# Keys, beta, gram products and block solve of the delta rule moved one period up, into a stream of their own

## The reference, cut to what matters

```python
xn = layernorm(x)
# layer 0: delta rule (4 heads, dk 128, dv 32) beside a two-layer network
q, k, v = xn @ Wq, xn @ Wk, xn @ Wv; beta = sigmoid(xn @ Wb); g = xn @ Wg
k = k * rsqrt(sum(k * k) + 1e-12)
#   S_t = S_{t-1} + k_t (beta_t (v_t - k_t^T S_{t-1}))^T ;  o_t = q_t^T S_t
o = norm(o) * silu(g)
x = x + o @ Wo + ffn(xn)       # ffn: 2 layers of window-64 attention (8 heads) and a GELU MLP
xn = layernorm(x)
# layer 1: latent attention, 16 heads of 8, causal, beside 6 experts (top 2) and a shared expert
x = x + latent_attention(xn) + moe(xn)
```

## Time and profile before

| | |
|---|---|
| median of 3 runs | 2267.91 us (2267.54 to 2269.87) |
| profiled execution | 2270.01 us, span 2268.0 us |
| PE, PEld busy | 1957.7, 1291.3 us |
| DVE, ACT, POOL busy | 1401.9, 947.8, 824.7 us |
| mean granted TensorE clock | 0.91 |
| HBM traffic | 32 GB/s over the span |

### The profile page before, as it was taken

The page is one execution under the profiler, slowest core; times in us unless marked ns, Lnnn a source line. Parts: engine busy times, 40 slices in busy tenths (PEclk is TensorE's granted clock), DMA queues, the critical chain, the costliest instruction groups (busy, mean ns, idle before and its releaser), DMA issues. The chain is left out here.

```text
span 2268.0 us, 40783 instructions
## 1 busy us (share of the span) xinstructions
PE 1957.7 (86%) x15104; PEld 1291.3 (57%) x15104; DVE 1401.9 (62%) x3394; ACT 947.8 (42%) x2465; POOL 824.7 (36%) x823
## 2 busy tenths in 40 slices
PE   3797779998899988998899988998799988998686
PEld 1594448564685557654585557654585556754332
DVE  3553465775758756775757756775767847674442
ACT  1413442365424652265424643265514653264023
POOL 4506550444406541443506542353505442160000
PEclk9788898999899998999899998999999998999557
DMA  4200012100311012200302012100212012100200
GB/s 167 50 20 15 17 35 62 53 14 15 77 36 41 18 40 61 53 14 15 78 24 54 18 38 64 53 14 11 71 31 57 14 31 74 47 16 1 75 1 6
DMA packets 124820, 89.71 MB, mean 40 GB/s; under 512 B 42168, under 2 KB 111928, under 8 KB 124344
## 3 DMA queue, kind: packets, MB, share of 16 engines
q1 hardware_dynamic: 124016, 85.39, 14.0%
q0 software_dynamic: 320, 1.05, 0.1%
q10 hardware_dynamic: 288, 0.67, 0.1%
HBM read 46.84 MB, written 25.17 MB: 32 GB/s over the span
## 5 line engine op out<-in xcount | busy, mean ns | idle before, releaser
L1636 POOL TENSOR_TENSOR soft<-soft,prec 128x512 f32<-128x512 f32 x128 | 135.7, 1066 | 541.6 <-DVE prec L1295 540.5
L1163 ACT ACTIVATE shared<-bank 128x512 f32<-128x512 f32 (+1 forms) x384 | 202.7, 528 | 254.3 <-PE bank L931 252.3
L1447 DVE TENSOR_REDUCE nmx<-bank 128x1 f32<-128x512 f32 (+3 forms) x352 | 224.6, 638 | 105.3 <-PE bank L909 104.4
L1083 ACT ACTIVATE soft<-bank,nmax 128x128 f32<-128x128 f32 x512 | 180.2, 384 | 169.4 <-DVE nmax L1287 168.7
L1597 POOL TENSOR_TENSOR qk_rs<-qk_rs,minus_half 128x16 f32<-128x16 f32 x64 | 187.8, 2935 | 5.3
L930 PE MATMUL bank<-b_sb 128*128 128x128 bf16 x512 | 118.0, 231 | 41.6 <-ACT shared L1163 39.7
L931 PE MATMUL bank<-shared 75*128 75x384 bf16 (+3 forms) x512 | 149.5, 318 | 0.0
L621 PE MATMUL bank<-w_sb,hT 128*128 128x512 f32 x256 | 136.7, 620 | 8.7 <-DVE hT L1237 5.7
L909 PE MATMUL bank<-shared 72*128 72x256 bf16 (+3 forms) x512 | 135.9, 317 | 0.0
L1595 POOL TENSOR_SCALAR rs_f<-mv_f 128x4 f32<-128x4 f32 x24 | 5.6, 234 | 344.2 <-DVE mv_f L1226 344.2
L593 PE MATMUL bank<-c_sb,soft 128*128 128x128 f32 x608 | 106.3, 308 | 27.5 <-POOL soft L1636 22.4
(11 more groups left out here) (236 smaller groups left out, 4809.1 us busy)
## 6 DMA issues: line engine op xcount, KB each, us to landing
shared<-parts_dram SPq DMA_DIRECT2D x64, 288.0 KB
vm<-v_f SPq DMA_DIRECT2D x112, 128.0 KB, 2.3
parts_dram<-parts SPq DMA_DIRECT2D x96, 128.0 KB, 2.5
L_dram<-shared SPq DMA_DIRECT2D x32, 256.0 KB, 2.5
shared<-X_dram SPq DMA_DIRECT2D x32, 256.0 KB, 3.0
shared<-L_dram SPq DMA_DIRECT2D x32, 256.0 KB, 3.8
w_sb<-weights SPq DMA_DIRECT2D x1, 4167.0 KB, 21.2
x_tm<-x SPq DMA_DIRECT2D x8, 256.0 KB, 3.1
```

The lines of the kernel that those rows point to most:

```text
L1083: a = af(v4(p_sb, 2, 4)[:, j, g], place("fS", j)[:, g * P:(g + 1) * P], ACT.Exp, bias=nmax[:, at:at + 1], accum_out=psums[:, at:at + 1])
L1163: af(v4(PTm, 2, GROUP)[:, u % 2, i, 0:n], place("mST")[:, 0:n], ACT.Exp).then_inc(mexp_done, 1)
L1447: reduce(v3(nmx[:], HM)[:, h:h + len(heads), c], v3(place("mS")[:, 0:len(heads) * (c + 1) * P], len(heads)), AX, ALU.max, negate=True).the ...
L1636: tt(p, p, spread(prec[:, at:at + NPAIR], P), ALU.mult).then_inc(fnorm_done, 1)
```

## The change

A new stream e ("early") holds, for item p+1 in period p: the head (x load, layernorm, transpose), `k`, `krs`, `beta`, `kT`, `gram`, `solve` and `keep`. The delta stream of item p now begins with `qT` and `bg` and goes on with the inversion. Item 0's early steps stand alone before period 0, and period 7 has none. To live beside the latent attention, kT, kn and the blocks of the solve get tiles of their own outside `shared`, L is written into `the` (the experts' tile), and `k`, `beta`, `kT` and `gram` all use PSUM bank 3, each waiting for the readers of the one before. Beta is computed by four products of 4 columns with one tanh; the gate `bg` by four products into one bank with one tanh and one multiply. `xnT` of the next item is written in the middle of the period, and the shifted copy `hT` later, from `xnT` (`hcopy`). `qT`'s four copies come first on ACT. The zeroing of `X_dram` moves from POOL's queue to SP's, behind the weight loads. All five order strings are new. In the PE order the e steps stand so: `hT` between `seq_u(p,1)` and `seq_o(p,1)`; `k` to `gram` spread over the last 77 of 307 steps, with three `mST`, one `mPV`, `matg`, `aT` and `final` behind the last gram. `inv_v(p,0,0)` stands 14th instead of 53rd. On DVE, `solve` stands behind the last `matg` and ahead of `final` and of the next period's first `fS`; on SP, `solve` and `keep` stand ahead of `final`.

```diff
-STREAMS = "fbdacm"
+STREAMS = "fbdacme"
 def steps_front(b):
-    return s + (steps_head(b + 1) + steps_chunks(b + 1, 0, 0, AHEAD) if b + 1 < BATCH else [])
+    return s + ([("hcopy", b + 1)] + steps_chunks(b + 1, 0, 0, AHEAD) if b + 1 < BATCH else [])
+def steps_early(b):
+    s = (steps_head(b) if b else []) + [("k", b, c) for c in range(NT)] + [("krs", b), ("beta", b)] + [("kT", b, c) for c in range(NT)]
+    return s + [("gram", b, c) for c in range(NT)] + [("solve", b), ("keep", b)]
 def steps_delta(b):
-    s = [("k", b, c) for c in range(NT)] + [("krs", b)] + [("bg", b, c) for c in range(NT)]
-    s += [("kT", b, c) for c in range(NT)] + [("gram", b, c) for c in range(NT)]
-    s += [("qT", b, h) for h in range(H0)] + [("solve", b)]
+    s = [("qT", b, h) for h in range(H0)] + [("bg", b)]
...
-            "k": lambda c: c % 2, "bg": lambda c: c % 2, "kT": lambda c: c % 2, "G": lambda c: c % 2,
+            "k": lambda c: 3, "beta": lambda: 3, "kT": lambda c: 3, "G": lambda c: 3, "bg": lambda: 0,
...
+        kT, kn, blk = sb("kT", NT * T), sb("kn", NT * T), sb("blk", 3 * BLK * BLK)
+        Lx = the
...
                 def gram(b, c):
                     kc = v4(kT, NT, H0)[:, c]
-                    pe.wait_ge(kT_copied, NT * b + min(c + 3, NT))
-                    if c >= 2:
-                        pe.wait_ge(L_done, NT * b + c - 1)
+                    if c:
+                        pe.wait_ge(L_done, NT * b + c)
+                    else:
+                        pe.wait_ge(kT_copied, NT * (b + 1))
...
+                def hcopy(b):
+                    dve.wait_ge(head_copied, b + 1)
+                    if b:
                         dve.wait_ge(fv_psum, ch(b, 0, 0))
-                    nc.vector.tensor_copy(xnT[:], place("hT")[:])
-                    nc.vector.tensor_copy(hT[0:64, :], place("hT")[0:64, :])
-                    nc.vector.tensor_copy(hT[64:P, 1:T], place("hT")[64:P, 0:T - 1]).then_inc(head_copied, 1)
+                    shifted(hT, xnT).then_inc(hT_copied, 1)
...
                 def inv_load(b, c):
                     if c == 0:
-                        keep(b)
-                    sp.wait_ge(Xb_kept, 16 * (b + 1))
+                        sp.wait_ge(Xb_kept, 16 * (b + 1))
+                        if b:
+                            sp.wait_ge(oT0_copied, b)
+                        if b > 1:
+                            sp.wait_ge(mPV_psum, GROUPS * 3 * (b - 1))
```

More of the change, by code:

```diff
@@ L204, in period @@
     if p < 0:
-        return {s: steps_head(0) + steps_chunks(0, 0, 0, AHEAD) if s == "f" else [] for s in STREAMS}
+        first = {"f": steps_head(0) + [("hcopy", 0)] + steps_chunks(0, 0, 0, AHEAD), "e": steps_early(0)}
+        return {s: first.get(s, []) for s in STREAMS}
     early, late = p < BATCH, p > 0
@@ L215, in walk @@
         left = {s: collections.deque(x for x in steps if x[0] in parts) for s, steps in period(p).items()}
-        for s in ORDER[engine]:
+        for s in ORDER[engine] if p >= 0 else [s for s in STREAMS for _ in left[s]]:
             if left[s]:
@@ L294, in build @@
         warm, minus_half = sb("warm", 2), sb("minus_half", 16)
-        kss, krs, beta = sb("kss", NT * H0), sb("krs", NT * H0), sb("beta", NT * H0)
+        kss, krs, beta, bt = (sb(n, NT * H0) for n in ("kss", "krs", "beta", "bt"))
         oss, ors = sb("oss", NT * H0), sb("ors", NT * H0)
@@ L517, in _ @@
                 sp.dma_start(c_sb[:, early_c:], consts[:, early_c:]).then_inc(late_loads, 16)
+                sp.wait_ge(zeroed, 2)
+                for c in range(NT):
+                    sp.dma_start(in_dram(X_dram, c), v3(zeros, H0)).then_inc(X_zeroed, 16)
+                sp.wait_ge(X_zeroed, 16 * NT)
                 sp.wait_ge(setup_loads, 16 * 3)
@@ L1150, in delta_back @@
                     af(o_all, place("o")[:], ACT.Copy).then_inc(o_back, 1)
-                    af(kn[:, 0:T], place("o")[:], ACT.Square).then_inc(osq_done, 1)
+                    af(Vm[:, 0:T], place("o")[:], ACT.Square).then_inc(osq_done, 1)
                 def oT0_(b):
@@ L1375, in gram @@
                     for h in range(H0):
-                        m = stt(v4(L, 2, H0)[:, c % 2, h], v3(place("G", c)[:], H0)[:, h], beta[:, c * H0 + h:c * H0 + h + 1],
+                        m = stt(v4(Lx, 2, H0)[:, c % 2, h], v3(place("G", c)[:], H0)[:, h], beta[:, c * H0 + h:c * H0 + h + 1],
                                 C("strict"), ALU.mult, ALU.mult)
@@ L1499, in rope @@
                         dve.wait_ge(split_done, 2 * n)
-                    elif j == 0 and b:
-                        dve.wait_ge(fin_done, b)
+                    elif j == 0:
+                        for kept in L_kept:
+                            dve.wait_ge(kept, 32 * min(b + 2, BATCH))
+                        if b:
+                            dve.wait_ge(fin_done, b)
                     dve.wait_ge(mq_psum, 2 * n + j + 1)
@@ L1755, in final @@
                     sp.dma_start(out[b:b + 1].rearrange("a (t p) d -> p (a t) d", p=P), v3(fin[:], NT)).then_inc(out_stored, 16)
-                walk("SP", {"x_load": x_load, "fv": fv, "gram": gram, "solve": solve, "inv_load": inv_load,
+                walk("SP", {"x_load": x_load, "fv": fv, "gram": gram, "solve": solve, "keep": keep, "inv_load": inv_load,
                             "fetch": fetch, "send": send, "mrow": mrow, "final": final})
```

135 lines of the change are left out of this document (75 added, 60 removed).

## The result

The changed kernel takes 2165.45 us (median of 4 runs, 2163.34 to 2167.9). The kernel before took 2268.89 in 4 runs on the same chip. The ratio is 0.9544, with a 95% interval of 0.9528 to 0.9561. That is 103 us less. The forecast was 2190, with a range of 2125 to 2258. The profiled execution has a span of 2163.0 us, against 2268.0.

What follows compares the result with a forecast made beforehand. The prediction took full periods to be near PE's work, with a hole around the solve and small gaps elsewhere. 2268 - 77 - 21 + 20 = 2190, + 2.0 around the span = 2192, median 2.1 lower: 2190; range 2125 to 2258.

Steps and rivals of the forecast that it cites:

- full periods: Periods 1 to 6: 243.7 us each, 12.8 less than 256.5; six of them -77.
- item 0: Start of the run: early steps lose their cover, +17, item 1's early steps +3; in all +20, between +5 and +32.
- period 7: Period without stream e: part 2 stays and part 1 shrinks by 123 - 102, so -21.
- the last period: Only a, c and m with their own chains: 0, between -4 and +4 from the new order.
- hole around the solve: In full periods PE is near its work but idles around DVE's solve; it stands still 4.3 us at 602.
- part 1: Full period before stream a's first score products: 123 us to 102; products -11.7, clock -4.5, idle 6 instead of 10.9.
- the 4 us allowed: Idle ahead of the inversion in part 1: 2 us for the X load, 2 more for DVE held by the solve.
- Part 2: Full period from stream a's first score products: 133.9 us to 141.7; 12.3 of products added, idle 8 instead of 12.5.
- more room: Rival: part 2 takes the early products without lengthening, staying 133.9 us; period 236, time 2144; chance 0.16.
- the hole only moves: Rival: the solve holds DVE uncovered, part 1 stays 111 us; period 253, time 2255; chance 0.19.
- X_dram's zeroing: Start of the run, zeroing behind the weight loads on SP's queue: 0, at worst +5.
- The bank: Rival: early steps' turns on PSUM bank 3 stall PE; period 268, time 2336; chance 0.13.

Runs made afterwards that it cites:

- e1: Kernel before, with DVE's solve cut from 30 chained operations to 2: 2225.54 us, ratio 0.9814.
- e8: Changed kernel, old orders in the last period and in period 7 from the first `mS` step, DVE's solve of items 0 and 1 later: 2151.8 us.
- e5: Changed kernel, with all 13 early steps at the very end of their period on all engines: 2459.92 us, ratio 1.0832.
- e9: Changed kernel, with 5.3 us of keys and transpose products a period taken out for items 1 to 7, turns kept: 2158.11 us, ratio 0.9513.
- e3: Changed kernel, with every keys product issued twice: 2189.37 us, ratio 0.9656 to the kernel before.
- e2: Changed kernel, with DVE's solve cut to its first row: 2148.67 us, ratio 0.9472 to the kernel before.
- e10: Changed kernel, with item 0's early steps taken in turns with the first two chunks of f: 2153.76 us, ratio 0.9491.
- e7: Changed kernel, with DVE's solve of items 0 and 1 put behind later steps: 2167.22 us, ratio 0.9547.

## Why the prediction was right, and where it was off

The direction, the range and the mechanism held; the forecast was 25 us too high. In the profile's own time it was 2192 against 2165: full periods 33.8 less than forecast, item 0 6.3 less, period 7 7 more, the last period 5.9 more. So part of the nearness is luck: misses of 40 us one way and 13 the other set each other off.

*What bounds the kernel.* "In a full period the kernel is near PE's work, with a hole around the solve" stood. e1 prices the solve in the hole at 5.8 us a period. Another 7.2 are products that left a full stretch (11.7) for one that grew by 4.5. What is left of the idle time and the slow products of part 1, some 6 us, goes with the rest of the chain (its turns, store and fetch); no run takes this apart. When the experiments began I had changed my mind and held the hole for most of the gain; e1 refuted that.

*Part 1.* Forecast -21.1: products -11.7, clock -4.5, idle -4.9. Measured -23.1: -11.7, -5.0 and -6.4. That 1.5 more us of idle went is because `fPT` and the inversion waited for less than the 4 us allowed. The first inversion product came 14.7 us in, where 14 was forecast, behind products and not behind X. DVE was held until 6.0 us into the period in the kernel after (788 to 797.3, the next beginning at 791.3), as worked out. X was fetched 10.7 us in (802.02, below) and landed 13.6 us in, at 804.87, where 16 was forecast; PE took it at 806.20. So the load is covered with 1.3 us to spare. SP's queue after:

```profile
797.35 0.36 SPq L1745 DMA_DIRECT2D X_dram<-blk  x1
802.02 0.36 SPq L1756 DMA_DIRECT2D shared<-X_dram  x1
```

*Part 2, the term that was mis-sized.* Forecast +7.8 for 12.3 us of products; measured +4.5, against part 2 before, which is the old order without early steps. The new order by itself is slower (e8, period 7), and its gaps take nearly all of the early products: e5's part 2 and period 7's are no shorter without them, and e9 gains nothing. A part of this is the clock, which was lower wherever they were missing: 0.98 with them, 0.97 in e9, 0.95 in e5, 0.92 in period 7. Why it was lower there no run shows. The rival "more room" (part 2 as before) was right at the margin: it was wrong by those 4.5, I by 3.3. The Trainium skill's rule that weight loads tell better than products how near PE is to its limit (Perfetto Trace Analysis, Identifying the Most-Contended Engine) points the right way: weight loads filled 76 of 138 us here while products filled 127, and 12.3 us of products had cost under half their time. e3 shows its limit here: with the loads at 78 of 143 us, 4.2 more cost 3.4. Nor did the gaps fill as I had it: idle was 12.5 before and 11.1 after. What busy time says of part 2 can't be added up.

*Full periods together.* 19.4 less instead of 12.8: 2.1 from part 1, 3.3 from part 2, and 1.2 from the period taken as an example and a mean misread (256.9, set against 256.5, where the mean was 258.3; and 238.3 where it was 238.9).

*Period 1 was missed.* I counted six full periods. Item 1's early steps meet a half of item 0 that is itself late, so its solve starts 7 us after the period does; it lost 8.2 us to the others, with a hole of 9.93, 9.2 of it the solve's own (e2). That is the rival "the hole only moves", right for one period of seven.

*Period 7.* Forecast -21, measured -14.0. "Its part 2 stays" failed: the order string is shared, and without its filler it costs 5.9 (e8).

*Item 0.* The chain was worked out as 107 for an inversion that came at 109.23. But the 109.2 before, beside which it looked as long, was a misreading: that is the second chunk's product, and the first stood at 104.70 (above). So the chain is 4.5 us longer, and with its cover gone it shows as the hole of 10.23 us; the short solve gives 8.7 of item 0 back (e2). The lost cover was put at 17; the whole came out as 13.7 instead of 20. Idle time rose by 7.5 (255.30 - 193.88 = 61.4 now, 53.9 before), busy time by 5.5, for item 1's early products lie in it. e10 shows that 9.9 of it come from where the early steps stand, not from their length.

*The last period.* Forecast 0, between -4 and +4; measured +5.9, which is the order's 7 (the table above) less what the clock happened to give (0.61 against 0.60).

*X_dram's zeroing.* Taken at 0, at most 5. The first transposes start at 33.17 us instead of 32.6: +0.6, in the start of item 0 (50.60 against 49.90).

*The bank.* A chance of 0.13 for 2336. Its mechanism exists (34.1 us bare in e5, some of it clock), its condition didn't occur: 0.4 us of waits in a full period. The Trainium skill's advice to rotate independent groups through PSUM banks (Perfetto Trace Analysis, Matmuls) therefore mattered here at most where the groups follow each other directly; e5 had no kernel with rotating banks beside it.

Open: which gaps of part 2 took the early products, why 4.2 us more cost 3.4 when 5.3 less gained nothing, and what the 6 us or so of part 1 are that e1 leaves.

## What to carry to other kernels

A chain with short turns and a long wait at its end (grams, solve, store and fetch) belongs one period earlier, spread between steps of another stream: its turns, its single bank and its latency then cost next to nothing here (0.4 us of waits; a short solve gains 0.3 in a full period), and the stretch it left got shorter by its whole work and its hole. Price the first and the last periods by themselves: strings of steps that are right for the five periods in the middle lost 8 us in period 1, 6 in period 7 and 7 in the last, and another start and end took 33 us off the changed kernel. Before reordering the steps that wait behind a chain, look when the chain's last load lands: e7's order could win next to nothing. Where busy time says that a stretch is full, add and take away a few us of work in it before believing it.

## What was not expected of the hardware

The last period differs by up to 9 us between profiles with the same order in it (171.5 to 180.5, and 163.3 to 170.9). Its mean granted clock, 0.57 to 0.67, differs with it: the stretch runs at 1.2 GHz for most of its length. e2's and e7's, both with the new strings:

```profile
1967.30:2147.80 180.50, 128.26 (x517) 56.57 (x516) 64.39 (x162) 35.53 (x66) 1.61 (x2) 0.57 0.09 26
```

```profile
1986.20:2157.70 171.50, 115.67 (x517) 51.69 (x516) 64.27 (x162) 35.54 (x66) 1.61 (x2) 0.64 0.10 27
```

The instructions are the same in number; PE is busy 128 us in the one and 116 in the other. Such a stretch can hide, or feign, a change of some 9 us. And removing 5.3 us of products in e9 took 1.6 from PE's busy time: two kernels with equal busy time need not do equal work.
